# A graph layer on one core: the scan's 17th and 18th block in spare buffers, and scatters that begin one group later

## The reference

```python
h = relu(layernorm(x))                        # x: 100000 nodes x 64
z = concat([h[src], h[dst], edge_attr], -1)   # 25000 edges x (64 + 64 + 32)
e = sigmoid(z @ W_f + b_f) * softplus(z @ W_s + b_s)
message = segment_sum(e, src, 100000)         # src is not in order; nodes repeat
mean, var = message.mean(0), message.var(0)   # per feature, over all nodes
out = x + h + (message - mean) * rsqrt(var + 1e-5) * gamma + beta
```

## Time and profile before

| | |
|---|---|
| median of 3 runs | 1065.7 us (1065.66 to 1067.62) |
| profiled execution | 1066.78 us, its span 1065.1 us |
| edge stage, scan, output stage | about 0 to 850, 850 to 932, 932 to 1065 us |
| busy in the span: PE, DVE, ACT, POOL | 60%, 69%, 51%, 69% |
| moved by DMA | 176.07 MB, 165 GB/s on average |

### The profile page before, as it was taken

The page is one execution under the profiler, slowest core; times in us unless marked ns, Lnnn a source line. Parts: engine busy times, 40 slices in busy tenths (PEclk is TensorE's granted clock), DMA queues, the critical chain, the costliest instruction groups (busy, mean ns, idle before and its releaser), DMA issues. The chain is left out here.

```text
span 1065.1 us, 11028 instructions
## 1 busy us (share of the span) xinstructions
PE 640.8 (60%) x2458; PEld 462.4 (43%) x2458; DVE 734.3 (69%) x1547; ACT 540.2 (51%) x1181; POOL 731.5 (69%) x652
## 2 busy tenths in 40 slices
PE   0474766566556666655666566766666789944232
PEld 0253554444344455444444344544544578810000
DVE  3884767575757577675666665776666559799788
ACT  1264565555555565554545454664646564434332
POOL 6776787878787877777777777877878752340710
PEclk9955555655565556665555555555556589955555
DMA  8997553535353433424233333433333399899999
GB/s 317 405 377 273 129 123 78 125 75 124 75 125 89 92 56 84 86 56 86 59 83 60 80 60 81 85 59 81 85 56 58 35 375 368 298 292 425 413 405 379
DMA packets 88183, 176.07 MB, mean 165 GB/s; under 512 B 42575, under 2 KB 49299, under 8 KB 79699
## 3 DMA queue, kind: packets, MB, share of 16 engines
q1 hardware_dynamic: 35851, 115.32, 30.8%
q0 software_dynamic: 42880, 20.09, 16.0%
q10 hardware_dynamic: 9416, 40.29, 9.3%
HBM read 107.12 MB, written 68.53 MB: 165 GB/s over the span
## 5 line engine op out<-in xcount | busy, mean ns | idle before, releaser
L594 POOL DMA_INDIRECT m_buf<-in_x_dram,m_buf x384 | 367.2, 956 | 118.6 <-issue 108.5
L607 POOL DMA_INDIRECT msgs_dram<-sums,target x184 | 289.6, 1574 | 61.0 <-issue 55.5
L1171 PE MATMUL ps_all<-sums,m_last 128*128 128x64 f32 x920 | 195.5, 405 | 124.4 <-ACT m_last L1033 104.0
L1171 PEld LDWEIGHTS ps_all<-sums,m_last 128*128 128x128 f32 x920 | 188.0, 313 | 135.9 <-issue 110.7
L719 DVE TENSOR_REDUCE m_last<-late 128x24 f32<-128x1536 f32 (+1 forms) x49 | 85.3, 1741 | 87.8 <-ACT late L984 87.8
L1131 PE MATMUL ps_all<-ident,m_buf 128*128 128x128 f32 x192 | 53.2, 433 | 125.8 <-DVE m_buf L809 125.8
L1145 PEld LDWEIGHTS ps_all<-m_buf 128*128 128x128 f32 x392 | 93.0, 326 | 49.5 <-issue 49.5
L794 DVE TENSOR_TENSOR target<-moved,m_last 128x4 int32<-128x4 f32 x49 | 9.6, 196 | 151.6 <-POOLq L605 151.3
L1033 ACT ACTIVATE m_last<-m_last,one_col 128x512 f32<-128x512 f32 x196 | 107.6, 550 | 1.6
L1131 PEld LDWEIGHTS ps_all<-ident,m_buf 128*128 128x128 f32 x192 | 35.2, 218 | 157.5 <-DVE m_buf L809 136.1
L1143 PE MATMUL ps_all<-m_buf 128*128 128x512 f32 x98 | 99.8, 1121 | 0.0
(11 more groups left out here) (171 smaller groups left out, 1080.0 us busy)
## 6 DMA issues: line engine op xcount, KB each, us to landing
m_buf<-msgs_dram SPq DMA_DIRECT2D x38, 1024.0 KB, 11.7
m_buf<-in_x_dram SPq DMA_DIRECT2D x48, 512.0 KB, 5.0
msgs_dram<-y_kept SPq DMA_DIRECT2D x14, 1536.0 KB, 11.4
out_dram<-m_buf ACTq DMA_DIRECT2D x20, 1024.0 KB, 11.0
m_buf<-src_rows_dram SPq DMA_DIRECT2D x47, 256.0 KB, 4.1
y_spill_dram<-y_kept ACTq DMA_DIRECT2D x19, 512.0 KB, 3.1
y_kept<-y_spill_dram SPq DMA_DIRECT2D x8, 1024.0 KB, 13.2
m_buf<-in_x_dram,m_buf POOLq DMA_INDIRECT x392, 2.5
```

The source lines that it names most:

```text
L594: pool.indirect_dma_start(xg[:, n % G_SLOTS, 2 * j + c, :], None, x, bass.IndirectOffsetOnAxis(ap=ids[:, c, n * TILES + j:n * TILES + j + ...
L607: pool.indirect_dma_start(msgs, bass.IndirectOffsetOnAxis(ap=target[:, n % UNROLL, j:j + 1], axis=0), comb[:, n % COMB_SLOTS, j, :], None, ...
L1171: pe.matmul(ps_c[:, j, :], same_of(b, j, j + 1)[:, 0, :], msg_of(g)[:, b, :], start=(b == 0 and not begun), stop=(b == j), skip_group_chec ...
```

## The change

Two constants and one function differ.

In stage one the scatters begin behind the gathers of the tenth group (n = 9) rather than the ninth, and there are three catch-up groups, 24, 32 and 40, rather than 24 and 40. 42 groups are scattered within the loop in both.

In stage two `scan_buf` maps blocks to buffers otherwise. Before: blocks 0 to 20 take buffers 0 to 4 in turn, and 21, 22, 23 take 5, 6, 7. After: blocks 0 to 15 take 0 to 4 in turn, 16 and 17 take 5 and 6, blocks 18 to 22 take 1, 2, 3, 4, 0, and 23 takes 7. So 18 comes into the buffer of 11 (before: of 13), 19 of 12, 20 of 13 (before: of 15), 21 of 14 and 22 of 15. The held blocks are the same and come in the same order.

```diff
-ACC_FIRST = 8
-CATCH_UP = (24, 40)
+ACC_FIRST = 9
+CATCH_UP = (24, 32, 40)
...
     def scan_buf(b):
 
-        first_new = NB - 1 - (M_BUFS - SCAN_BUFS)
-        return b % SCAN_BUFS if b < first_new else SCAN_BUFS + b - first_new
+        first_new, n_early = NB - 1 - M_BUFS, M_BUFS - SCAN_BUFS - 1
+        if b < first_new:
+            return b % SCAN_BUFS
+        if b < first_new + n_early:
+            return SCAN_BUFS + b - first_new
+        return (b - n_early) % SCAN_BUFS if b < NB - 2 else M_BUFS - 1
```

## The result

| | before | changed |
|---|---|---|
| median of 6 runs | 1067.45 us (1065.66 to 1068.32) | 1061.32 us (1060.81 to 1062.56) |
| profiled execution, span | 1066.78, 1065.1 us | 1060.81, 1059.1 us |
| scan's end (variance, L1757, now L1761) | 930.75 us | 925.54 us |
| from there to the end of the span | 134.35 us | 133.56 us |

The ratio is 0.9949, with an interval of 0.9939 to 0.9958: 0.5% faster, 5.4 us (the two medians are 6.1 us apart). All medians in this text are over fast runs: the one slow run, 1155.11 us in e4, is left out. The span is 6.0 us shorter, of which 5.2 are there when the variance is ready and 0.8 come after it.

The account below looks back on a forecast made before the run. GpSimd was taken to bound the edge stage, PE the scan's end, and DMA to be full in the output stage. Gains of 4.4 + 1.6 = 6.0 us took 1065.7 to 1059.7 us; 8-in-10 range 1057.0 to 1062.4.

Parts of the forecast that it names:

- GpSimd as the belt of stage one: Edge stage: GpSimd sets the pace; closing its 4.97 us hole before the first scatter gains 4.4 us.
- The 0.25 us that I charged for one more catch-up: Extra catch-up at group 32: one stall 0.25 us over the usual gap, taken off the 4.7 us gain.
- upper bound of 4.7: Edge stage: most that the later scatters could gain, 4.7 us, if no catch-up stalled.
- Nobody queued behind is hurt: Edge stage: gathers aren't held, and VectorE picks up some 10 us of shift with 32 us of idle cover.
- Loads asked for earlier: Scan: blocks 18 to 22 load earlier, DMA's hole of 896 to 908 fills, last load lands 4 us sooner.
- No gain for the scan: Scan: PE, not data, sets 901.5 to 929, so the earlier loads gain nothing there.
- The worth in the output stage: Output stage: two late scatters leave the stretch where DMA is full, worth 1.6 us; bounds nothing and 4 us.
- The sum: Whole kernel: 4.4 + 1.6 = 6.0 us saved, span 1059.1 us, median of runs 1059.7 us.
- the rival's 1061.3: Whole kernel: time if only GpSimd's 4.4 us counts and the earlier loads buy nothing; chance 0.28.
- The earlier loads buy nothing: Rival, output stage: the scatters' freed work sinks into idle time, leaving 1061.3 us; chance 0.28.
- they buy 4 us: Rival, output stage: the loads' full 4 us head start reaches the end, giving 1057.3 us; chance 0.12.
- The slower case, PE's clock: Rival, scan: PE's clock stays low from block 16 on, costing 9.6 us, giving 1069.3 us; chance 0.03.

Follow-up runs that it names:

- e4: The changed kernel run again unaltered, as control beside its parts; median 1061.05 us, ratio to before 0.9942.
- e1: The kernel before with only the new scatter order, scan buffers as before; median 1062.22 us, ratio to before 0.9948.
- e9: The changed kernel run a third time unaltered, as control of the third batch; median 1061.19 us, ratio to before 0.9945.
- e2: The kernel before with only the new scan buffers, scatter order as before; median 1066.45 us, ratio to before 0.9995.
- e7: The changed kernel with scatters beginning behind the eleventh group's gathers and four catch-up groups (20, 26, 32, 40); median 1060.87 us, ratio to before 0.9946.
- e8: The changed kernel with PE waiting for VectorE's message sum and clearing the banks behind block 15 instead of 13; median 1059.34 us, ratio to before 0.9932.
- e10: The kernel of e8 again: the changed kernel with PE's clearing behind block 15 instead of 13; median 1059.48 us, ratio to before 0.9933.
- e11: The kernel of e10, but with the scan's buffers as before the change; median 1059.95 us, ratio to before 0.9936.
- e5: The changed kernel with the late groups' scatters held until PE has crossed the last block; median 1065.36 us, ratio to before 0.9986.
- e6: The changed kernel without the twelve late scatters, their semaphore raised instead; median 1060.10 us, ratio to before 0.9939.
- e3: The changed kernel with the late groups' scatters held until PE has crossed block 22; median 1063.57 us, ratio to before 0.9965.
- e12: The kernel of e3 again: the changed kernel, late scatters held until block 22 is crossed; median 1060.46 us, ratio to before 0.9948.

## Why the prediction came out as it did

**GpSimd as the belt of stage one: right.** The forecast was 4.4 us with bounds to 4.7, the last scatter of stage one is 4.98 us earlier, and e1 shows that this part alone carries the gain to the end. The 0.25 us that I charged for one more catch-up is the term that was off: the stall isn't a fixed price. It was 0.25 at group 24 before, 0.08 there after (0.22 and 0.11 in e4 and e9, the same kernel, and nothing in e1), and nothing at groups 32 and 40. The 4.98 us lie above the upper bound of 4.7, part of which is that less was stalled at group 24 than before, which no bound of mine allowed for. The remaining 0.1 us I can't place; the hole itself was 1.2 us longer in e2's execution, so no such remainder can be read from two profiles. The rule of the Trainium skill that I had weighed (DMA: Bandwidth & Descriptors, Anatomy of one DMA — SWDGE (gpsimd) path: about 2 us fixed, longer with HBM targets) would have given no stall. The trace shows none at two of three catch-ups, and 0.08 us at the third, so its sum of 4.7 was the nearer one, if not for its reason: at group 24 the report still took as long as half a group of gathers, 5 us.

**Nobody queued behind is hurt: right.** The gathers wait for nothing but the issue gap (118.7 us idle before 384 of them, 109.4 of it named so), and VectorE is back at waits near 4 us after each catch-up. e7 shows the same at an even greater distance.

**Loads asked for earlier: right, 3.45 us against 4 forecast,** with the issues in the order and places that were worked out. VectorE's waits for reloads fell by 0.5 to 1.0 us, where 1 to 3 were forecast.

**No gain for the scan: right.** PE's run is 14.33 us in both, and e8 and e10 move the scan's end by touching PE alone.

**The worth in the output stage: right mechanism, wrong size.** The step was "two scatters give 1.2 to 1.6 us; I take 1.6". Measured are 0.8 us in the two profiles and 0.5 us over the means (133.84 against 134.34, the mean of before and e1). Compared only among profiles whose clock did the same, it is 0.65 us with the fall (before and e1 against changed and e9) and 0.6 without it (e11 against e10). That is near what two of the late scatters cost if one costs 0.27, and also near what SP's wait costs when it ends 2.5 us sooner, by the table under e5; which of the two it is stays open. I had priced a scatter by DMA's busy share in a window in which DMA was lightly loaded, 0.6 us, and by the excess share in a full one, 0.8. e6 gives 0.1 to 0.27 us. Such a share isn't capacity used: it stands at up to 1.12 in windows that move less (380 GB/s) than windows at 1.01 (420 GB/s), so an excess of share can't be turned into time. e5 shows the other half, which the sum left out: what the late scatters can cost is also SP's wait for them.

**The sum.** 6.0 us were forecast, the span gave 6.0 and the ratio 5.4: stage one's term was 0.6 too small and the output's 0.8 to 1.1 too large. That the sum is so near is luck: the two errors cancel. The forecast of 1059.7 was set against the median of the first three runs; over all six that median is 1067.45, not 1065.7, and these 1.75 us are the whole distance to 1061.32 (1.6 us). That the measured time lies on the rival's 1061.3 is an accident of the same kind.

**The rivals.** "The earlier loads buy nothing" was nearer than "they buy 4 us". The slower case, PE's clock, did not take place as a loss against before, but it lives in both kernels. In the profiles of before, changed, e1, e5 and e9 the 112 crossings took 14.40 us, in those of e2, e3, e4, e6, e7 and e12 12.77. That is 1.63 us, by which executions of one kernel differ (changed and e9 against e4). The two profiles of the result both have the fall, so it isn't in their difference.

## What to carry to other kernels

When one in-order engine is busy nearly without a break, look for the few real holes in its own order of time, and move independent work of the same queue in front of the wait that makes the hole; the gain is the hole, and more distance brought nothing here. Filling a hole in DMA is worth only what waits behind its last transfer: find who sets the end of the stretch before pricing it, and don't price small transfers by their busy share. Where an engine that sets the end of a stretch waits for another's result only to do housekeeping, do the housekeeping later.

## What the hardware showed that I had not expected

- GpSimd's sequencer runs well ahead of its engine. VectorE was released at 98.62 us by a semaphore that stands in the program behind the tenth group's eight gathers, and the last of these began at 102.84; the scatter behind it began at 104.09.
- A pause of 0.94 us of PE, with a light clearing after it, was followed in five of eleven profiles by a stretch at half clock (0.72 on average over four microseconds in the changed kernel), worth 1.63 us. Without the pause (e8, e10, e11) the clock stayed up in three of three, and the runs' spread was 0.7 to 0.8 us (changed kernel and e7: 1.1 to 2.4). That the pause brings the fall is likely by this and not shown: six of eleven profiles with the pause have no fall either.
- Twelve indirect scatters with addition, each of 128 rows of 256 bytes, cost the output stage 1.1 us in all (e6), 0.1 to 0.27 us for one, while one that is nearly alone in its window shows 0.6 us of DMA share.
- DMA's share can rise while its rate falls: 1.12 at 380 GB/s (944 to 948) against 1.01 at 420 (891 to 895 in the changed kernel).
